# Wide attention scored in pairs of heads: half-height matmuls, halves of PSUM banks, and a new order of the work

## What is computed

```python
# second layer, wide attention, per batch b: h is (1024, 256)
qkv = h @ W_qkv + b_qkv                # Q, K, V: 16 heads x 64 features
scores = Q @ K.T / 8                   # per head, 1024 x 1024
attn = softmax(where(causal, scores, -inf))
y = (attn @ V) @ W_out + b_out
```

## Time and profile before

| | |
|---|---|
| median of 3 runs (lowest, highest) | 6034.55 us (6022.65, 6040.91) |
| the profiled execution | 6037.1 us |
| its span, first to last instruction | 6035.3 us |
| mean granted TensorE clock | 0.856 |
| wide attention, batches 0 to 2, with ticks beside | about 577 us each |
| wide attention, batch 3, without ticks | about 410 us |

### The profile page before, as it was taken

One profiled execution on the slowest core, in us unless ns is written; L12 is line 12 of the kernel. 1 busy time (PEld: TensorE's weight loads), 2 busy tenths in 40 slices (PEclk: granted clock), 3 DMA queues, 4 the chain that ended last, 5 costly groups with the idle time before them and its releaser, 6 DMA issues. The chain is left out here.

```text
span 6035.3 us, 83328 instructions
## 1 busy us (share of the span) xinstructions
PE 4555.1 (75%) x30341; PEld 2907.5 (48%) x30341; DVE 4105.7 (68%) x8455; ACT 2766.3 (46%) x6047; POOL 1904.3 (32%) x1563
## 2 busy tenths in 40 slices
PE   4454478888677778888777678888867686999776
PEld 2333345656434454566533454666633353566334
DVE  6999957777886656777787655777788565322630
ACT  2343315666253533666445351666435360455333
POOL 2555512434322421344333440343423341000001
PEclk7666689999787889999888788999978798999888
DMA  3000000000202120000121112000031101000312
GB/s 122 11 11 25 1 22 24 18 13 15 51 17 76 39 89 21 16 13 9 42 37 59 45 54 68 12 13 12 15 53 36 65 31 50 17 10 9 62 60 72
DMA packets 113334, 213.59 MB, mean 35 GB/s; under 512 B 25729, under 2 KB 70633, under 8 KB 109553
## 3 DMA queue, kind: packets, MB, share of 16 engines
q1 hardware_dynamic: 104736, 190.94, 11.5%
q0 software_dynamic: 6144, 16.79, 0.9%
q10 hardware_dynamic: 2048, 0.53, 0.0%
HBM read 154.38 MB, written 49.73 MB: 34 GB/s over the span
## 5 line engine op out<-in xcount | busy, mean ns | idle before, releaser
L1490 DVE MAX8 vals<-work 128x8 f32<-128x128 f32 (+7 forms) x1536 | 1080.4, 743 | 0.4
L1864 POOL TENSOR_SCALAR keep<-ssb,vals 128x128 bf16<-128x128 f32 (+7 forms) x512 | 876.2, 1724 | 0.0
L467 PE MATMUL ring<-ident,pr 128*128 128x128 f32 x2304 | 479.2, 327 | 455.5 <-POOL pr L1869 389.8
L1851 POOL TENSOR_TENSOR pool_step<-ones 128x2 f32<-128x2 f32 x256 | 49.9, 195 | 2333.4 <-DVE vals L1490 2324.5
L1504 DVE MATCH_REPLACE8 work<-vals,work 128x128 f32<-128x128 f32 (+7 forms) x1024 | 750.7, 739 | 0.0
L574 PE MATMUL pA<-SC 128*128 128x512 f32 (+3 forms) x1536 | 632.9, 522 | 121.5 <-ACT SC L1202 96.0
L1869 POOL TENSOR_TENSOR pr<-keep,pr 128x128 f32<-128x128 bf16 (+7 forms) x512 | 647.9, 1287 | 0.0
L467 PEld LDWEIGHTS ring<-ident,pr 128*128 128x128 f32 x2304 | 324.4, 167 | 614.4 <-POOL pr L1869 424.9
L1141 ACT ACTIVATE prT<-ring 128x512 f32<-128x512 f32 (+1 forms) x768 | 381.0, 498 | 451.7 <-PE ring L467 449.8
L1619 DVE TENSOR_REDUCE nmax<-pA 128x1 f32<-128x1024 f32 (+7 forms) x512 | 382.0, 749 | 266.4 <-PE pA L575 255.8
L1490 DVE MAX8 vals<-ssb 128x8 f32<-128x128 f32 (+7 forms) x512 | 362.9, 750 | 241.1 <-ACT ssb L1129 218.7
(11 more groups left out here) (225 smaller groups left out, 8049.2 us busy)
## 6 DMA issues: line engine op xcount, KB each, us to landing
SC<-in_w SPq DMA_DIRECT2D x64, 512.0 KB, 6.9
stage<-parts SPq DMA_DIRECT2D x384, 64.0 KB, 2.4
parts<-SC SPq DMA_DIRECT2D x72, 256.0 KB, 4.2
SC<-parts SPq DMA_DIRECT2D x144, 128.0 KB, 7.8
SC<-in_wqkv SPq DMA_DIRECT2D x32, 384.0 KB, 2.9
rows_out<-SC SPq DMA_DIRECT2D x92, 128.0 KB, 1.7
SC<-rows_in SPq DMA_DIRECT2D x20, 512.0 KB, 3.9
SC<-in_ffn_we SPq DMA_DIRECT2D x4, 2048.0 KB, 10.0
```

The lines of the kernel that those rows point to most:

```text
L467: mm = pe.transpose(r[:, blk % 4 * P:blk % 4 * P + P], pr0[:, p % 2, blk * P:blk * P + P], ident[:, :])
L1490: m = v.max(vals0[:, y, i, 8 * n:8 * n + 8], src[:, lo:hi])
L1864: pool.tensor_scalar(keep0[:, lo:hi], ssb0[:, p % 2, lo:hi], vals0[:, p % 2, i, TOPK - 1:TOPK], None, ALU.is_ge).then_inc(s["k"], 1)
```

## The change

Three things are changed in wide attention.

1. **Q and scores.** ScalarE writes Q once (`qT`, 128 rows, one instruction in the place of two), and the zeros that GpSimd wrote are gone. The scores of a pair of units are issued together: for each chunk of up to 512 columns a matmul over rows 0 to 63 into pA[1], then one over rows 64 to 127 into pA[0]; then both masks.
2. **Halves of the banks.** Pairs with tiles of up to 4 blocks use columns 0 to 511 or 512 to 1023 of both pA by turns (`columns`). `free` says how many exponentials must be done before a pair's scores may start, `ahead` which pairs' scores are issued at pair p (0 and 1 before the loop, 6 and 7 both at 5).
3. **The order.** TensorE: `turn` of unit 2p, scores of the pairs of `ahead(p)`, `turn` of unit 2p + 1, `values` of pair p - 1, the ticks of both units. ScalarE: both exponentials of pair p, both `turned`, `out_of_psum` of pair p - 1, the ticks. VectorE: the row maxima of the pairs of `ahead(p)`, then the ticks.

```diff
+    def columns(self, u):
+        i, _ = self.unit(u)
+        lo = 512 if i < 4 and u // 2 % 2 else 0
+        return lo, lo + (i + 1) * P
+
+    def ahead(self, p):
+        return {-1: (0, 1), 0: (), 5: (6, 7), 6: (), 7: ()}.get(p, (p + 1,))
+
+    def free(self, p):
+        return {0: 0, 1: 0, 7: 12}.get(p, 2 * p)
...
-                def scores(G, u):
-                    i, j = WD.unit(u)
+                def scores(G, p):
+                    i, _ = WD.unit(2 * p)
                     w = (i + 1) * P
-                    if u >= 2:
-                        pe.wait_ge(s["e"], G * 16 + u - 1)
-                    p = pA[(u + 1) % 2]
+                    if WD.free(p):
+                        pe.wait_ge(s["e"], G * 16 + WD.free(p))
+                    c0, _ = WD.columns(2 * p)
                     for lo in range(0, w, 512):
                         hi = min(lo + 512, w)
-                        pe.matmul(p[:, lo:hi], qm[:, j, i * P:i * P + P], kT[:, lo:hi], start=True, stop=(hi < w))
-                    pe.matmul(p[:, w - P:w], identm[:, :], tri[:, 1, :], start=False, stop=True).then_inc(s["s"], 1)
+                        for u in (2 * p, 2 * p + 1):
+                            rows = slice(u % 2 * 64, u % 2 * 64 + 64)
+                            pe.matmul(pA[(u + 1) % 2][:, c0 + lo:c0 + hi], qT[rows, i * P:i * P + P], kT[rows, lo:hi],
+                                      start=True, stop=(hi < w))
+                    for u in (2 * p, 2 * p + 1):
+                        pe.matmul(pA[(u + 1) % 2][:, c0 + w - P:c0 + w], identm[:, :], tri[:, 1, :], start=False,
+                                  stop=True).then_inc(s["s"], 1)
...
-                    scores(G, 0)
+                    pe.wait_ge(s["eqk"], G * 2 + 2)
                     pe.wait_ge(s["ev"], G + 1)
-                    scores(G, 1)
-                    for u in range(16):
-                        if u + 2 < 16:
-                            scores(G, u + 2)
-                        turn(G, u)
-                        if u % 2 and u >= 3:
-                            values(G, u // 2 - 1)
-                        at("wide", g * 17 + 1 + u)
+                    for q in WD.ahead(-1):
+                        scores(G, q)
+                    for p in range(8):
+                        turn(G, 2 * p)
+                        for q in WD.ahead(p):
+                            scores(G, q)
+                        turn(G, 2 * p + 1)
+                        if p:
+                            values(G, p - 1)
+                        for u in (2 * p, 2 * p + 1):
+                            at("wide", g * 17 + 1 + u)
...
-                    for j in range(2):
-                        rows = slice(j * 64, j * 64 + 64)
-                        act.activation(qm[rows, j, :], pA[0][rows, :], ACT.Identity, scale=0.125,
-                                       bias=bq_s[rows, :]).then_inc(s["eqk"], 1)
+                    act.activation(qT, pA[0][:, :], ACT.Identity, scale=0.125, bias=bq_s[:, :]).then_inc(s["eqk"], 1)
...
-                    exponential(G, 0)
-                    for u in range(16):
-                        if u + 1 < 16:
-                            exponential(G, u + 1)
-                        turned(G, u)
-                        if u % 2 and u >= 3:
-                            out_of_psum(G, u // 2 - 1)
-                        at("wide", g * 17 + 1 + u)
+                    for p in range(8):
+                        for u in (2 * p, 2 * p + 1):
+                            exponential(G, u)
+                        for u in (2 * p, 2 * p + 1):
+                            turned(G, u)
+                        if p:
+                            out_of_psum(G, p - 1)
+                        for u in (2 * p, 2 * p + 1):
+                            at("wide", g * 17 + 1 + u)
...
-                    rowmax(G, 0)
-                    rowmax(G, 1)
-                    for u in range(16):
-                        if u + 2 < 16:
-                            rowmax(G, u + 2)
-                        at("wide", g * 17 + 1 + u)
+                    for p in range(-1, 8):
+                        for q in WD.ahead(p):
+                            rowmax(G, 2 * q)
+                            rowmax(G, 2 * q + 1)
+                        if p >= 0:
+                            for u in (2 * p, 2 * p + 1):
+                                at("wide", g * 17 + 1 + u)
...
-                pool.memset(qm, 0.0).then_inc(s_qz, 1)
```

More of the change, by code:

```diff
@@ L312, in build @@
         prT = cut(0, 4096).rearrange("p (a n) -> p a n", n=N)
-        qm = cut(4096, 2048).rearrange("p (j n) -> p j n", j=2)
+        qT = cut(4096, N)
         kT = cut(6144, N)
@@ L360, in build @@
         s_out = sem("s_out")
-        s_qz = sem("s_qz")
         s_rf = sem("ring_filled")
@@ L624, in wide @@
                         spread(G - 1)
-                    pe.wait_ge(s["eqk"], G * 3 + 2)
+                    pe.wait_ge(s["eqk"], G * 2 + 1)
                     for t in range(NT):
@@ L631, in wide @@
                     at("wide", g * 17)
-                    pe.wait_ge(s["eqk"], G * 3 + 3)
-                    scores(G, 0)
+                    pe.wait_ge(s["eqk"], G * 2 + 2)
                     pe.wait_ge(s["ev"], G + 1)
-                    scores(G, 1)
-                    for u in range(16):
-                        if u + 2 < 16:
-                            scores(G, u + 2)
-                        turn(G, u)
-                        if u % 2 and u >= 3:
-                            values(G, u // 2 - 1)
-                        at("wide", g * 17 + 1 + u)
+                    for q in WD.ahead(-1):
[9 more added lines that the diff above has]
+                            at("wide", g * 17 + 1 + u)
                 values(b * 8 + 7, 7)
@@ L957, in wide @@
                         sp.wait_ge(a1["ev"], G + 1)
-                        sp.wait_ge(a1["eqk"], G * 3 + 3)
+                        sp.wait_ge(a1["eqk"], G * 2 + 2)
                         group_weights(g + 1)
@@ L1197, in exponential @@
                 def exponential(G, u):
-                    w = (WD.unit(u)[0] + 1) * P
+                    lo, hi = WD.columns(u)
                     if u == 0 and G >= 2:
@@ L1201, in exponential @@
                     act.wait_ge(s["mx"], G * 16 + u + 1)
-                    act.activation(pr[:, u % 2, 0:w], pA[(u + 1) % 2][:, 0:w], ACT.Exp,
+                    act.activation(pr[:, u % 2, 0:hi - lo], pA[(u + 1) % 2][:, lo:hi], ACT.Exp,
                                    bias=nmax[:, u % 4:u % 4 + 1],
@@ L1211, in turned @@
                         act.activation(prT[:, u % 4, c * 512:c * 512 + w], r[:, 0:w], ACT.Copy).then_inc(s_re, 1)
-                act.wait_ge(s_qz, b + 1)
+                act.wait_ge(pj[0]["dr"], min(b + 2, B) * 192)
                 for g in range(8):
@@ L1618, in rowmax @@
                         v.wait_ge(s["e"], G * 16 + u - 3)
-                    v.tensor_reduce(nmax[:, u % 4:u % 4 + 1], pA[(u + 1) % 2][:, 0:w], AX, ALU.max,
+                    v.tensor_reduce(nmax[:, u % 4:u % 4 + 1], pA[(u + 1) % 2][:, lo:hi], AX, ALU.max,
                                     negate=True).then_inc(s["mx"], 1)
@@ L1951, in _ @@
                 norm("n1", b)
-                pool.wait_ge(pj[0]["dr"], min(b + 2, B) * 192)
-                pool.wait_ge(s_x, b * 16 + 16)
-                pool.memset(qm, 0.0).then_inc(s_qz, 1)
                 norm("n2", b)
```

## The result

The changed kernel takes 6397.7 us (median of 4 runs, 6394.4 to 6406.7) against 6035.0 us: the ratio is 1.060, 95% interval 1.059 to 1.062. Slower was forecast, by 2.3%; it is 6.0%. The time lies in the widest stated range, 6040 to 6430 us, but outside the 6080 to 6300 to which the forecast itself gave 0.62, and the growth is 363 us where the sum gave 139.

A forecast was written before the change was run, and what follows sets the result against it. TensorE was taken to bound wide attention without ticks, VectorE to be close to full with ticks between projections. 6037.1 + 21 without ticks + 118 with ticks gave 6176, stated as 6175 us; own range 6080 to 6300, widest 6040 to 6430.

The forecast's parts named there:

- TensorE bounds the stage without ticks: Wide attention of the last batch: TensorE, busy 389 of 410 us against VectorE's 108, sets the time.
- full overlap of halves of rows: Scores in wide attention: the two heads' half-height matmuls run at the same time, saving 7.6 us a group.
- the stall behind ScalarE's order: Before each pair's transposes TensorE waits while ScalarE copies values and makes the exponential: 8.1 us a group.
- the last batch: Wide attention without ticks: savings and added waits sum to +2.6 us a group, +21 us in 8 groups.
- the wait with ticks: TensorE's waiting added to each group with ticks: the 8.1 us stall plus terms of 5.6 and 3.0 us.
- The terms of 5.6 and 3.0: Groups with ticks: ScalarE ending its ticks late, 5.6 us; its `topk` exponentials waiting for VectorE's first maxima, 3.0 us.
- The changes of shape: TensorE switching between full-height work and half-height scores: 0.15 us each, two for each of 8 pairs, 2.4 us a group.
- VectorE's floor: Groups with ticks: VectorE's work plus its 14.1 us wait for V's projection allow no less than 68.6 us.
- faster rival: Wide attention: TensorE saves more than it waits if it waits under 0.79 us a pair; 5909 us, chance 0.11.
- the sum with ticks: Groups with ticks: 51.3 + 2.6 + 14.5 + 5.6 + 3.0 = 77.0 us against 72.1, +118 us in 24 groups.
- No overlap: Scores in wide attention: half-height matmuls queue, +7.6 us in each of 32 groups; 6418 us, chance 0.14.
- Cover on ScalarE: Groups with ticks: ScalarE keeps up, leaving only the stall without ticks; 6058 us, down to 6040, chance 0.13.

The follow-up runs named there:

- e5: Kernel before, in its own order, each score matmul over its head's 64 rows alone, one unit at a time: 6287 us, 1.042 of the kernel before.
- e3: Changed kernel with two unused float32 matmuls added behind the ticks of pairs 1 to 6, in batches with ticks: 6251 us, 1.036 of the kernel before.
- e4: Changed kernel with scores again at full height, against Q with zeros; pairs, half banks and new order stay: 6501 us, 1.078 of the kernel before.
- e2: Changed kernel with ScalarE's exponentials of the next pair ahead of the ticks, still behind the copy of the values: 6139 us, 1.017 of the kernel before.
- e6: Changed kernel with both exponentials of the next pair ahead of the copy of the values on ScalarE: 6045 us, 1.002 of the kernel before.
- e7: e6 with the ticks of unit 2p again between the two units on TensorE and ScalarE: 6000 us, 0.994 of the kernel before.
- e8: e2 with scores at full height, against Q with zeros: 6277 us, 1.040 of the kernel before.
- e10: e7 with scores at full height, against Q with zeros: 6131 us, 1.016 of the kernel before.
- e9: e7 with one unused float32 matmul ahead of the first transposes of pairs 1 to 7, in batches with ticks: 6002 us, 0.994 of the kernel before.
- e1: Changed kernel with ScalarE's exponential of unit u + 2 right behind the copy of unit u's transposes: 6112 us, 1.013 of the kernel before.

## Why the prediction was wrong in size

**Right, or nearly.** That TensorE bounds the stage without ticks; full overlap of halves of rows (scores 152.5 to 79.3 us); the stall behind ScalarE's order (8.1 us a group forecast, 64.5/8 = 8.1 measured); the last batch (50.6 + 2.6 = 53.2 us from one group to the next, against 52.9); the wait with ticks (8.1 + 5.6 + 3.0 = 16.7 us forecast, 139.0/8 = 17.4 measured) as a sum. The terms of 5.6 and 3.0 were not measured each by itself, and the longest wait holds 2.63 us of DMA issues that the forecast does not name. The changes of shape were mis-sized, 0.15 for 0.075 us each (1.2 us a group less than I took); the sum still fitted, so about as much is missing elsewhere in it, which was not traced. The Trainium skill ("TensorEngine Tiling (Array Packing)", Key Properties) has the array drained at a change of mode; e5 agrees that halves of rows pay, with little. The Trainium skill ("TensorE: Matmul & The Clock Gate", "Why this matters for your kernels") gives 3.07 times for four row groups of 32; for two halves of 64 rows the trace here has all of it: 768 columns of both heads in 1.56 us (L591), where one head took 1.46 to 1.56.

VectorE's floor of 68.6 us a group was misread, which touches only the lower bound and the faster rival. The wait of 14.1 us for the projection of V is that of one group. Over the 8 groups of the first batch, before the change, it is this:

```profile
DVE SC L1632 <- PE pA L628: 95.7, 8, 16.6
```

That is 12.0 us a group, and the floor 436/8 + 12.0 = 66.5 us.

**Wrong: the sum with ticks.** The step that failed is that TensorE's work keeps its price. The sum read TensorE's 14.5 us of ticks, and all of its other work, from stretches at a clock of 0.96 and kept them, while it added 16.7 us of waiting to every group. The balance of one batch in the changed kernel: without ticks TensorE is busy 347.5 us; the ticks add 505.1 - 389.4 = 115.7; together 463.2, at the old clock. Measured are 532.9. The 69.7 us between are 8.7 us a group, at a clock of 0.85. The group was forecast at 77.0 us and took 87.0: 8.7 of the 10 us are that one term. The rest is 0.7 us more wait for the exponential and small change. e3 confirms its size from the other side (53 us of it won back by filling). The same balance, each kernel's first batch against its own last one, leaves 35 us in e4 (clock 0.91), 25 in e2 and 26 in e6 (0.92), 18 in e7 (0.93), 15 in e8 (0.94), 3 in e10 (0.96) and, less the filling, 17 in e3 (0.93) and 1 in e9 (0.96). e1 and e5 are left out, whose last batches do not run at the full clock. The lower the clock, the more TensorE's busy time grows, whatever the order of the lists and the height of the matmuls.

**Why the clock fell** is shown in part. Two things go with it: waiting (e3 fills it and the clock goes from 0.85 to 0.93; e2 takes most of it away: 0.92) and half-height work (e4 takes it away and leaves the waits: 0.91; e5 has it alone, with TensorE always busy: 0.83 in the last batch; e8 and e10 without it: 0.94 and 0.96). Taking away either one brings back more than half of the fall from 0.96 to 0.85, so they act together, and how they share the 69.7 us stays open. Nor are they enough: the last batch of the changed kernel has both, 56 waits of 1.15 us in the mean and the half-height pairs, and its clock is 1.00. With ticks the waits are longer (2.2 us in the mean, 5.5 the longest) and the ticks' own matmuls stand between; no run tells which of these is needed.

**The rivals.** *No overlap* (6418 us) would have met the time within 20 us, by luck; the row of L591 excludes it: 79.3 us in the last batch, and e4 is 103 us slower. *Cover on ScalarE* did not happen: the wait is 17.4 us a group. *Faster* put its point of decision at 0.79 us of wait a pair; it was 1.15. e6 and e7 show part of that side of it: they leave 28 of the 64.5 us of the wait in the last batch, and it is 22 us shorter than before where 44 were forecast. With ticks they get a group to 72 us (e7), no lower. In e7 VectorE is busy 439.8 of 575.6 us and waits 95.3 for the projection of V, 66.9 us a group together. Of the other 5 us it waits 3.9 for scores; what holds these up was not traced.

## What to carry to other kernels

When a new order makes one engine issue both of a pair early, go through the other engines' lists and ask what stands directly ahead of the step that the first will wait for; here two exponentials moved on ScalarE take 6.0% of loss to 0.2%, and the finer ticks to a gain of 0.6%. Where a change makes TensorE wait or do narrower work, do not carry its durations over from the old clock: price them at both levels, and look first at the granted clock of the new stretch. Work added in TensorE's gaps tells whether its clock costs time: in the changed kernel it won 49 us a batch (e3), in e7 nothing (e9).

## What was not expected of the hardware

Half-height matmuls, one at a time between full-height work, lower TensorE's granted clock though the engine is busy 97% (e5: 0.71 to 1.00 from group to group of the same work, 53 to 69 us). Two of them on different halves of the rows run fully beside each other, float32 and 512 columns included (152.5 to 79.3 us for all scores of a batch). And adding some 82 us of unused matmuls to a batch made it 49 us shorter.
